# A local-attention stack on one core: the softmax division and the turn of the probabilities move to VectorE, the outputs come out of TensorE already turned, and the values are shifted inside SBUF

## The reference, cut to what matters

```
def local_attention(q, k, v):              # 16 heads of 64, windows of 32 tokens
    bq = q.reshape(b, h, nw, w, d)
    bk2, bv2 = look(bk), look(bv)          # each window sees itself and the window before: 64 keys
    sim = einsum('bhwie,bhwje->bhwij', bq, bk2) * QK_SCALE
    sim = where(mask, -max, sim)
    attn = softmax(sim, -1)
    out = einsum('bhwij,bhwje->bhwie', attn, bv2)
    return out.reshape(b, h, n, d)
x = attn_layer(shift_tokens(x), Wqkv[i], q_scale[i], k_scale[i], Wo[i]) + x
x = ffn_layer(shift_tokens(x), ln_g[i], ln_b[i], W1[i], b1[i], W2[i], b2[i]) + x
```

## Time and profile before

| what | value |
|---|---|
| median of 3 runs | 4365.75 us (4363.63 to 4371.05) |
| span of the profiled execution | 4366.1 us |
| TensorE, weight loads | 90%, 63% of the span |
| VectorE, ScalarE, GpSimd | 63%, 61%, 69% |
| first stack, second stack | 222 to 1870 us, 2016 to 3655 us |
| chain that ended last | TensorE 38%, no other engine over 4% |

### The profile page before, as it was taken

The page is one execution under the profiler, slowest core; times in us unless marked ns, Lnnn a source line. Parts: engine busy times, 40 slices in busy tenths (PEclk is TensorE's granted clock), DMA queues, the critical chain, the costliest instruction groups (busy, mean ns, idle before and its releaser), DMA issues.

```text
span 4366.1 us, 169503 instructions
## 1 busy us (share of the span) xinstructions
PE 3908.6 (90%) x69444; PEld 2744.4 (63%) x69444; DVE 2756.9 (63%) x4939; ACT 2682.7 (61%) x5560; POOL 3002.4 (69%) x1858
## 2 busy tenths in 40 slices
PE   7889999999999999977999999999999998265975
PEld 5556666676666766744766666666666665153645
DVE  5566666676766666734667676677676764623751
ACT  5657666676666767644676666767666675133752
POOL 0088888888888888814988888888888884611011
PEclk9999999999999999979999999999999998577987
DMA  2033433434334344311344343443433432031004
GB/s 68 2 86 90 112 97 95 110 93 107 97 95 104 96 105 102 93 46 42 96 102 104 92 111 93 103 108 92 108 98 96 108 92 55 0 104 27 2 13 127
DMA packets 349837, 367.90 MB, mean 84 GB/s; under 512 B 58738, under 2 KB 285299, under 8 KB 348787
## 3 DMA queue, kind: packets, MB, share of 16 engines
q1 hardware_dynamic: 338834, 348.59, 31.4%
q0 software_dynamic: 2048, 4.20, 0.3%
q10 hardware_dynamic: 8160, 3.93, 0.3%
HBM read 246.79 MB, written 109.71 MB: 82 GB/s over the span
## 4 chain that ended last, share of the span: by engine, by line
PE 38%; DVE 4%; ACT 4%; issue 3%; POOL 2%; DMA 1%; DVEq 0%; POOLq 0%; ACTq 0%
PE banks L328 6%; PE banks L356 4%; PE banks L369 4%; PE banks L416 3%; PE banks L460 3%; PE banks L312 2%; PE banks L295 2%; PE banks L401 2%; PE banks L454 1%; PE banks L386 1%; PE banks L1382 1%; ACT arena L996 1%; PE banks L1402 1%; DVE arena L619 1%; PE banks L923 1%
## 5 line engine op out<-in xcount | busy, mean ns | idle before, releaser
L690 POOL TENSOR_TENSOR arena<-arena 128x512 f32<-128x512 f32 x768 | 959.6, 1270 | 414.6 <-DVE arena L619 235.2
L695 POOL TENSOR_TENSOR arena<-arena 128x1024 f32<-128x1024 f32 x384 | 906.0, 2359 | 30.1
L692 POOL TENSOR_TENSOR arena<-arena 128x1024 f32<-128x1024 f32 x384 | 907.5, 2363 | 0.0
L619 DVE SCALAR_TENSOR_TENSOR arena<-arena,banks 128x512 f32<-128x512 f32 x768 | 493.5, 684 | 503.8 <-ACT arena L502 500.9
L328 PE MATMUL banks<-w_qk,arena 128*128 128x512 f32 x1536 | 734.5, 601 | 16.0 <-DVE arena L719 10.6
L470 ACT COPY arena<-banks 128x512 f32<-128x512 f32 x384 | 224.3, 584 | 656.8 <-PE banks L416 656.7
L612 DVE TENSOR_REDUCE arena<-arena 128x8 f32<-128x512 f32 x768 | 494.0, 679 | 86.1 <-ACT arena L486 84.2
L486 ACT ACTIVATE arena<-banks 128x512 f32<-128x512 f32 x768 | 441.3, 593 | 62.5 <-PE banks L328 50.5
L416 PE MATMUL banks<-ident,arena 128*128 128x128 f32 x3072 | 425.3, 282 | 28.6 <-POOL arena L695 20.5
L328 PEld LDWEIGHTS banks<-w_qk,arena 128*128 128x128 f32 x1536 | 276.4, 193 | 271.4 <-issue 271.4
L586 DVE TENSOR_REDUCE arena<-banks 128x8 f32<-128x512 f32 x384 | 264.0, 687 | 212.5 <-PE banks L312 212.1
(11 more groups left out here) (217 smaller groups left out, 6519.4 us busy)
## 6 DMA issues: line engine op xcount, KB each, us to landing
v_rows<-arena SPq DMA_DIRECT2D x1536, 64.0 KB
arena<-v_rows SPq DMA_DIRECT2D x768, 128.0 KB
arena<-v_rows SPq DMA_DIRECT2D x768, 112.0 KB
arena<-in_moe_w SPq DMA_DIRECT2D x30, 515.5 KB, 3.8
w_qk<-in_stack_qk SPq DMA_DIRECT2D x48, 256.0 KB, 3.0
w_v<-in_stack_v SPq DMA_DIRECT2D x48, 128.0 KB, 3.3
w_o<-in_stack_o SPq DMA_DIRECT2D x12, 512.0 KB, 3.9
w_w<-in_stack_w SPq DMA_DIRECT2D x12, 341.0 KB, 3.1
```

What stands on the lines that cost most here:

```text
L619: last = nc.vector.scalar_tensor_tensor(qn[:, :, tile], rn, 1e12, bank(M, tile).rearrange("p (h q d) -> p h q d", h=GH, q=2), ALU.min, ALU ...
L690: nc.gpsimd.tensor_tensor(f.sined[:, :, :, half, :], x[:, :, :, 1 - half, :], sines[:, :, mine].unsqueeze(1).to_broadcast([D, GH, 4, DH // ...
L692: nc.gpsimd.tensor_tensor(rot, x.rearrange("p h t a d -> p h t (a d)"), cosines.unsqueeze(1).to_broadcast([D, GH, 4, DH]), ALU.mult).then_ ...
L695: nc.gpsimd.tensor_tensor(rot, rot, f.sined.rearrange("p h t a d -> p h t (a d)"), ALU.add).then_inc(S.rotated, 1)
```

## The change

Four things change in a step of the stack, and nothing outside it.

1. VectorE divides the probabilities before they are used, not the outputs after: the product with the inverse sum now reads and writes the tile `p` in SBUF (L559 of the new kernel), and the product out of the banks (L596) goes. The sum, the reciprocal, the division and the turn follow the subtraction without another unit's work between them.
2. VectorE turns the probabilities in blocks of 32x32 with one instruction (L562); TensorE's four transposes (L401) and ScalarE's copy out of bank 6 go.
3. The outputs are formed with the values as the loaded operand and the turned probabilities as the streamed one, so they come out with features on the partitions. There are 64 products of 32 contracted rows, 64 loaded columns and 32 streamed columns, into banks 3 to 6 (L366); the 32 products (L312) and the four transposes of the outputs (L386) go. The block stands behind the projection of q and k, not behind the scores.
4. The values keep a ring of four tiles, and a copy shifted by 32 partitions is made by two DMAs from SBUF to SBUF; the way over DRAM with eight DMAs goes.

```
@@ pe_stack_step
-    if st.on(4):
-        u = s - 4
-        st.wait(S.probs_taken, u + 1)
-        pe.wait_ge(S.v_loaded, st.n64 + 64 * (u + 1))
-        st.wait(S.normed, u)
-        ...
-                    last = pe.matmul(bank(M, 4 + par)[c:c + 32, o:o + DH], f.pt[r, win // 4, hp, c:c + 32],
-                                     f.vb[r, u % 2, win, hp, :], start=True, stop=True)
-        last.then_inc(S.outs, 1)
...
+    pe_stack_outs(M, st)
+    pe_stack_values(M, st)
+    if s % G != 3:
         pe_stack_hidden(M, st, 1)
-        pe_stack_probs_turned(M, st)
-        pe_stack_outs_turned(M, st)
...
+def pe_stack_outs(M, st):
+    pe, s, S, f = st.eng, st.s, M.st, stack_buffers(M)
+    if st.on(4):
+        u = s - 4
+        st.wait(S.probs_turned, u + 1)
+        pe.wait_ge(S.v_loaded, st.n32 + 32 * (u + 1))
+        if st.on(3):
+            st.wait(S.shifted, u + 2)
+        st.wait(S.heads_taken, u + 3 if st.on(2) else u + 2 if st.on(3) else u + 1)
+        st.wait(S.outs_taken, u)
+        pe.sem_inc(M.s.pe_waited)
+        for hp in range(2):
+            for tile in range(2):
+                o = (2 * hp + tile) * WIN
+                for half, v in ((1, f.vt), (0, f.vp)):
+                    for g in range(4):
+                        r = slice(32 * g, 32 * g + 32)
+                        for par in range(2):
+                            last = pe.matmul(bank(M, 3 + g)[64 * par:64 * par + 64, o:o + WIN],
+                                             v[r, u % V_RING, tile, par, DH * hp:DH * hp + DH],
+                                             f.pt[r, u % 2, 4 * tile + 2 * hp + par, half, :],
+                                             start=(half == 1), stop=(half == 0), skip_group_check=True)
+        last.then_inc(S.outs, 1)
@@ dve_stack_step
         st.wait(S.scores, u + 1)
-        st.wait(S.outs, u)
...
-    if st.on(4):
-        u = s - 4
-        st.wait(S.outs, u + 1)
-        st.wait(S.inverted, u + 1)
-        st.wait(S.outs_turned, u)
-        nc.vector.tensor_tensor(f.o.rearrange("p (x b) d -> p x b d", b=2), two_banks(M, T, DH),
-                                f.inv.rearrange("p (x b) -> p x b", b=2).unsqueeze(3).to_broadcast([D, 4, 2, DH]),
-                                ALU.mult).then_inc(S.normed, 1)
-    if st.on(3):
-        u = s - 3
         st.wait(S.probs, u + 1)
         nc.vector.tensor_reduce(f.total, f.p, AX.X, ALU.add).then_inc(S.summed, 1)
         st.wait(S.summed, u + 1)
-        st.wait(S.normed, u)
         nc.vector.reciprocal(f.inv, f.total).then_inc(S.inverted, 1)
+        st.wait(S.inverted, u + 1)
+        nc.vector.tensor_tensor(f.p, f.p, f.inv.unsqueeze(2).to_broadcast([D, 8, KW]), ALU.mult).then_inc(S.normed, 1)
+        st.wait(S.normed, u + 1)
+        st.wait(S.outs, u - 1)
+        nc.vector.transpose(f.pt[:, u % 2].rearrange("p x h q -> p (x h q)"),
+                            f.p.rearrange("p x k -> p (x k)")).then_inc(S.probs_turned, 1)
@@ sp_stack_values
-    for w4 in range(4):
-        ...
-        sp.dma_start(M.v_rows[b].rearrange("a j (t w) c -> w j t a c", t=2)[w4], f.vt[r, b]).then_inc(S.v_stored, 16)
...
+    sp.dma_start(f.vp[WIN:D, b], f.vt[0:D - WIN, b]).then_inc(S.v_loaded, 16)
+    sp.dma_start(f.vp[0:WIN, b, 1], f.vt[D - WIN:D, b, 0]).then_inc(S.v_loaded, 16)
```

More of the change, by code:

```diff
@@ L225, in pair_steps @@
     n2 = eng.snap(n * 2)
-    n64 = eng.snap(n * 64)
+    n32 = eng.snap(n * 32)
     for s in range(steps):
-        step(M, Step(eng, m, layer, pair, s, (n, n2, n64), f, mode))
+        step(M, Step(eng, m, layer, pair, s, (n, n2, n32), f, mode))
 def unit_steps(M, eng, m, step):
@@ L278, in pe_stack_step @@
         st.wait(S.shifted, u)
-        st.wait(S.normed, u - 1)
+        st.wait(S.outs_taken, u - 1)
         pe.sem_inc(M.s.pe_waited)
@@ L365, in pe_stack_values @@
         u, g = s, s % G
-        st.wait(S.heads_taken, u - 1)
+        st.wait(S.v_taken, u)
         for tile in range(2):
@@ L410, in pe_stack_heads @@
         st.wait(S.outs_taken, u - 2)
-    else:
-        st.wait(S.v_taken, u + 2 if st.on(1) else u + 1)
+        st.wait(S.heads_taken, u)
     for hp in range(2):
@@ L415, in pe_stack_heads @@
             o = hp * T + tile * 128
-            last = pe.transpose(bank(M, 2 if qk else 3)[:, o:o + 128],
+            last = pe.transpose(bank(M, 6 if qk else 3)[:, o:o + 128],
                                 f.rot[:, u % 2, 2 * tile + qk, 2 * hp:2 * hp + 2, :], M.ident[:])
@@ L477, in act_stack_step @@
         st.wait(S.probs_turned, u)
-        st.wait(S.summed, u)
         nc.scalar.activation(f.p, f.zs, ACT.Exp, scale=8.0).then_inc(S.probs, 1)
@@ L513, in act_stack_values @@
         st.wait(S.v, u + 1)
-        if not (st.first and u < 2):
-            act.wait_ge(S.v_stored, st.n64 + 64 * (u - 1))
-        nc.scalar.copy(f.vt[:, u % 2].rearrange("p t a c -> p (t a c)"), bank(M, 2)).then_inc(S.v_taken, 1)
-def act_stack_probs(M, st):
-    S, f, nc, u = M.st, stack_buffers(M), M.nc, st.s - 3
-    if st.on(3):
-        st.wait(S.probs_turned, u + 1)
-        st.wait(S.outs, u)
-        nc.scalar.copy(f.pt.rearrange("p t h k -> p (t h k)"), bank(M, 6)).then_inc(S.probs_taken, 1)
+        st.wait(S.outs, u + 1 - V_RING)
+        nc.scalar.copy(f.vt[:, u % V_RING].rearrange("p t a c -> p (t a c)"), bank(M, 2)).then_inc(S.v_taken, 1)
 def act_stack_outs(M, st):
@@ L530, in act_stack_outs @@
         u = s - 4
-        st.wait(S.outs_turned, u + 1)
+        st.wait(S.outs, u + 1)
         if u % G == 0 and not (st.first and u == 0):
             act.wait_ge(S.projected, st.f * 2 + u // G)
-        nc.scalar.copy(stack_hidden(M).ot[:, u % G].rearrange("p h t -> p (h t)"), bank(M, 3)).then_inc(S.outs_taken, 1)
+        nc.scalar.copy(stack_hidden(M).ot[:, u % G].rearrange("p h (t g q) -> p (h t) g q", t=2, q=WIN),
+                       four_banks(M)).then_inc(S.outs_taken, 1)
 def act_stack_hidden(M, st, place):
```

83 lines of the change are left out of this document (16 added, 67 removed).

## The result

The changed kernel takes 4919.43 us (median of 4 runs, 4911.94 to 4922.49) against 4364.69 us, a ratio of 1.126 with a 95% interval of 1.125 to 1.128: 12.6% slower. The forecast was 4850 us with a range of 4610 to 5120.

What follows compares the result with a forecast made beforehand. TensorE was taken to bound the kernel at 8.56 us a step. With VectorE's chain at 9.33, a pair takes 78.4 us against 68.5: 9.9 x 48 = 475, about 10 for tables, 4366 + 485 = 4850 us; range 4610 to 5120.

Steps and rivals of the forecast that it cites:

- The wait at GpSimd: VectorE's division L559, both inputs in SBUF, waits about 1.9 us for GpSimd's running instruction; mean about 2.2 us; chance 0.80.
- Rival A: At the division L559: no wait at GpSimd; VectorE's step 7.39 us, 4265 us in all, down to 4118; chance 0.10.
- The turn: VectorE's 32x32 block transpose behind the division: taken as 0.69 us, between 0.20 and 1.22, without a wait.
- Rival B: VectorE's turn contends with GpSimd too: 2.1 us a step, 800 us more, 5650 us; chance 0.05.
- The ordinary step: VectorE's chain from one scaling's end to the next, wait included: 9.33 us, whatever TensorE does.
- The long steps: Beyond eight ordinary steps, a pair gets 1.27 us of feed-forward instructions and 2.46 at the GELU: 78.4 us against 68.5.
- rival C: TensorE bounds after all: 64 products over 2.9 us, or its clock falls; some might show, 4850 to 5200 us; chance 0.05.
- The step with the GELU: Once a pair GELU keeps ScalarE 4.41 us, so the division waits for GpSimd's next instruction: 2.46 us more.
- The rest hides: Beside VectorE's chain, TensorE (63.3 of 78.4 us a pair), ScalarE's copies, DMAs and GpSimd's own work add no time.
- my upper bound of 1.56: TensorE's block of 64 products: 24 ns per instruction gives 1.56 us from above, 0.78 from below; 1.0 was taken.
- What TensorE gains: TensorE's step loses 1.65 us and gets 1.0; pair 63.3 us, 250 us less in all if TensorE stayed the bound.
- ScalarE loses one copy and moves another: ScalarE's queue in a step: one copy goes and another moves, counted among what hides, at no cost.

## Why the prediction was right, and where its reasons were not

**The wait at GpSimd: right.** It exists (mean 2.05 us, forecast about 2.2; minimum 0.69, forecast 0.7), it follows the length of GpSimd's instruction, it goes with the second input's place, and alone it costs 211 us in the kernel before. Taking it away from the changed kernel brings 276 us. Rival A, no wait, is refuted. Behind a division that met its third, GpSimd's fourth instruction was held by 0.33 us, less than the half microsecond forecast.

**The turn: right.** 0.711 us, never stretched, where I took 0.69. Rival B is refuted. The estimate of 0.71 us, worked out from the 311 ns in the Trainium skill, VectorE: DVE Perf Modes, section The three transpose paths, agrees with the trace.

**The ordinary step: right.** 9.18 and 9.29 us in the rows above, and 9.30 as the median of all steps but those with the GELU, forecast 9.33. One of its terms was read off a near row: the 0.09 us before the end of scaling is the start of an L651, not of a maximum.

**The long steps: too short.** The pair takes 79.7 us against 78.4, 62 of the 69 us that the forecast was short of the time. Most of it are third and fourth steps of a pair: 24 of these 96 take 10.7 to 12.0 us, each with a standstill of 2.0 to 3.6 us, and they put some 57 us on the run. The clock has a part in it: five third steps with such a standstill, after which L433 kept its 2.74 us, stayed at 9.3 us. This is the clock fall that rival C kept open at 4850 to 5200, though not from the gaps of waiting that I had in mind. The step with the GELU takes 12.2 us on average, where 9.33 and 2.46 make 11.8.

**"The rest hides": wrong.** Two terms failed. A block of 64 products takes 1.41 us and not 1.0, near my upper bound of 1.56, and TensorE stands still in it 102 us in all; I counted its columns and not its instructions. So a step of TensorE gains 1.65 - 1.41 = 0.24 us and not 0.65, and the 250 us of "What TensorE gains" are not there: it is busy 3908.6 us before, 4072.1 in the changed kernel (in part at the lower clock) and 3974.9 with the inverse in PSUM. Its share of the stacks fell to 87% and not to about 80%, and of its forecast waits those for the feed-forward and the heads came, that for `scaled` hardly.

And "ScalarE loses one copy and moves another" was costed at nothing without asking what stands behind that copy in ScalarE's queue: the inverse. The changed kernel covers both, since VectorE's row is a little longer; so the forecast's time came out while its account was too simple.

Without the wait I expected 4265 us and 4644 came: I had put 585 us on the wait, and the runs give it 211 to 276. The other half of the loss, 276 us, is there without it. Half the products take 159 us of it away, mostly in the steps with a standstill, while the wait for the inverse shrinks by 148; the rows show how a standstill reaches the scaling, by way of the block, the copy and the inverse. That the copy held the inverse is shown, for the wait fell to its own 0.55 us when the order was turned; what that cost is not, since both runs with that order were slower.

**Open.** With neither the wait nor half of the products 117 us (2.7%) are left against the kernel before; that run has a wait of TensorE's values for the division that I added (213.7 us in all, and 36.1 us in the run with all products), so it bounds the rest from above only. No version with all of the products was faster than the kernel before; of those of the new design the inverse in PSUM is the fastest, 5.6% below the changed kernel.

## What to carry to other kernels

Before putting an elementwise product of two SBUF tiles on VectorE beside a busy GpSimd, count a wait until the end of GpSimd's running instruction, or give the product one input in PSUM. When an instruction is moved in an engine's queue, price what stands behind it, and what frees its buffer: the copy of the outputs was short and costly on either side of the inverse. And a forecast that hits can still have its loss in the wrong place: only the run without the named cause showed how much was left.

## What the runs showed of the hardware

- TensorE stands still for up to 3.6 us within rows of small products, with no semaphore to wait for, and goes on 1.1 to 1.6 us after a packet of instructions has landed: 65 times and 102 us in the block of 64 products of the changed kernel, 58 times and 52 us in the 32 of the kernel before, which follow 32 others, never within the block with half the products or with 32 larger ones. After the one in the rows above it worked at the 1.2 GHz level.
- 64 products of 32 contracted rows, 64 loaded and 32 streamed columns take 1.41 us, 22 ns each; 32 with 128 loaded and 64 streamed columns take 1.95 us, 61 ns each, so that joining them gained nothing.
- A turn of 128 by 512 float32 in blocks takes 0.711 us beside a busy GpSimd as without it, and 0.669 us right behind another turn of the same tile.
